# A wait of TensorE for its own transposes, and other places for three steps of VectorE and GpSimd in block 1

## The reference

```python
x = _layernorm(x + attention(x))          # first half, not touched
n = SU_ug.shape[0]
y = fwht(x * SU_ug) / SCALE               # 512-wide Hadamard transform of the tokens
up   = y @ W_up.T   * (Wscale_ug[:INTER] * SCALE)
gate = y @ W_gate.T * (Wscale_ug[INTER:] * SCALE)
y = fwht(silu(gate) * up * SU_dp) / SCALE # 2048-wide Hadamard transform
y = y @ W_down.T * (Wscale_dp * SCALE)
x = _layernorm(x + y)
```

## Time and profile before

| | |
|---|---|
| median of 3 runs | 1532.14 us |
| lowest, highest | 1530.12, 1534.98 us |
| the profiled execution, whole | 1534.02 us |
| its span, first to last instruction | 1532.2 us |
| mean granted TensorE clock | 0.997 |
| TensorE busy with matmuls | 1488.6 us, 97% |
| VectorE, ScalarE, GpSimd busy | 75%, 47%, 47% |

### The profile page before, as it was taken

How to read it: one execution, slowest core, us unless ns; L and a number is a source line. 1 busy time by engine, 2 the same in 40 slices (tenths; PEclk the granted TensorE clock), 3 DMA queues, 4 the chain that set the end, 5 groups by cost and what they waited for, 6 DMA issues and landing times.

```text
span 1532.2 us, 30672 instructions
## 1 busy us (share of the span) xinstructions
PE 1488.6 (97%) x11420; PEld 1394.1 (91%) x11420; DVE 1148.4 (75%) x1948; ACT 725.3 (47%) x1485; POOL 727.6 (47%) x861
## 2 busy tenths in 40 slices
PE   6999999999999999999999999999999999999998
PEld 4977988887887889899989999999999999999998
DVE  6776787677687886887886787688678677677665
ACT  4254245236227755444444455455455445545543
POOL 5465457438347553556663273264263254245122
PEclk9999999999999999999999999999999999999999
DMA  7022022122113797589779899899989988988981
GB/s 287 1 99 88 35 83 104 36 83 104 65 56 111 267 354 265 213 322 342 291 255 348 311 319 331 315 311 343 337 296 319 368 277 299 379 303 288 338 319 66
DMA packets 119298, 357.26 MB, mean 233 GB/s; under 512 B 12912, under 2 KB 13296, under 8 KB 117360
## 3 DMA queue, kind: packets, MB, share of 16 engines
q1 hardware_dynamic: 118144, 351.09, 63.5%
q10 hardware_dynamic: 1008, 4.20, 0.7%
HBM read 297.58 MB, written 57.67 MB: 232 GB/s over the span
## 4 chain that ended last, share of the span: by engine, by line
PE 58%; DVE 6%; issue 2%; ACT 2%; DMA 1%; POOL 1%; DVEq 0%; POOLq 0%; ACTq 0%
PE ff_acc L2517 16%; PE ff_bank_b L2486 16%; PE ff_bank_a L2486 10%; PE ff_bank_c L2486 10%; PE ff_acc L2551 1%; DVE ff_hs_a L2123 1%; PE ff_acc L2554 1%; DMA ff_pair_l<-low_scratch 1%; PE ff_x_ps L2445 1%; PE ff_x_ps L2434 1%; PE ff_x_ps L2457 1%; DVE ff_pair_l L2099 1%; PE ff_acc L2542 1%; DVE fb_h_lo L2118 1%; ACT at_union L601 1%
## 5 line engine op out<-in xcount | busy, mean ns | idle before, releaser
L2486 PE MATMUL ff_bank_b<-ff_x_hi,ff_ring 128*128 128x256 f32 x1536 | 299.1, 279 | 1.3 <-issue 0.6
L2486 PEld LDWEIGHTS ff_bank_b<-ff_x_hi,ff_ring 128*128 128x128 f32 x1536 | 247.8, 189 | 2.2 <-issue 1.8
L2486 PE MATMUL ff_bank_b<-ff_x_lo,ff_ring 128*128 128x256 f32 x768 | 214.2, 279 | 0.0
L1718 POOL TENSOR_TENSOR ff_h_sum<-ff_hf 128x256 f32<-128x256 f32 x54 | 40.6, 752 | 353.4 <-DVE ff_hf L2111 353.4
L2517 PE MATMUL ff_acc<-ff_pair_h,ff_hs_a 128*128 128x256 f32 x1080 | 201.4, 282 | 7.1 <-DVE ff_hs_a L2123 4.8
L2486 PE MATMUL ff_bank_a<-ff_x_hi,ff_ring 128*128 128x256 f32 x1024 | 201.5, 281 | 1.1 <-DVE ff_hf L2111 1.1
L2486 PE MATMUL ff_bank_c<-ff_x_hi,ff_ring 128*128 128x256 f32 x1024 | 202.0, 282 | 0.0
L2517 PEld LDWEIGHTS ff_acc<-ff_pair_h,ff_hs_a 128*128 128x128 f32 x1080 | 170.4, 190 | 9.2 <-DVE ff_hs_a L2123 5.8
L2486 PEld LDWEIGHTS ff_bank_c<-ff_x_hi,ff_ring 128*128 128x128 f32 x1024 | 165.3, 189 | 2.1 <-issue 2.1
L2486 PEld LDWEIGHTS ff_bank_a<-ff_x_hi,ff_ring 128*128 128x128 f32 x1024 | 165.3, 189 | 1.7 <-issue 1.6
L1883 ACT ACTIVATE ff_sg<-ff_c,h_ug_scale 128x512 f32<-128x512 f32 (+1 forms) x128 | 76.7, 614 | 158.7 <-DVE ff_c L2221 144.0
(11 more groups left out here) (369 smaller groups left out, 4243.2 us busy)
## 6 DMA issues: line engine op xcount, KB each, us to landing
ff_ring<-gu_scratch SPq DMA_DIRECT2D x392, 512.0 KB, 5.4
gu_scratch<-ff_ring SPq DMA_DIRECT2D x56, 512.0 KB, 4.3
ff_pair_l<-low_scratch SPq DMA_DIRECT2D x96, 256.0 KB, 3.7
ff_pair_more<-low_scratch SPq DMA_DIRECT2D x65, 256.0 KB, 3.6
at_xt<-in_xt SPq DMA_DIRECT2D x4, 2048.0 KB, 8.3
at_xn<-in_x SPq DMA_DIRECT2D x32, 256.0 KB, 2.9
x_scratch<-at_x SPq DMA_DIRECT2D x32, 256.0 KB, 2.0
fb_raw<-in_wgu SPq DMA_DIRECT2D x8, 1024.0 KB, 6.9
```

Of the source, the lines that this page charges most:

```text
L1718: pool.tensor_tensor(s1, a21, a22, ALU.add).then_inc(sum_s, 1)
L2486: i = pe.matmul(bank[:, m, :], r[:, a, m, c, :], b[:, k, c, :], start=(k < 3 and m == 0 and c == 0 and b is x_hi and a == 0), stop=(m == 1 ...
```

## The change

Three things are done. First, behind each turn of x in blocks 1 to 6 TensorE waits for the semaphore that the last of its own four transposes raises (24 places: six blocks, four turns). Second, GpSimd does `combine_down(2)` behind the sums of step 2 instead of ahead of the lo part for group 0, and `combine_down(3)` behind the three lo parts for group 2 instead of ahead of the one for group 1; the counts in `wd_summed` and `h_summed` follow. Third, VectorE makes the last lo part of the right operand of groups 0 to 3 (`lower_pair(q, 6)`) ahead of the first lo part of the left operand of the next group, instead of behind it.

```diff
         def wd_summed(n):
-            return sum_s, 4 * PAIRS + n + (0, 0, 8, 16)[(n - 1) // 4]
+            return sum_s, 4 * PAIRS + n + (0, 0, 12, 20)[(n - 1) // 4]
 
         def h_summed(n):
-            return sum_s, 4 * PAIRS + n + (8, 12, 16)[min((n - 1) // 8, 2)]
+            return sum_s, 4 * PAIRS + n + (8 if n <= 12 else 12 if n <= 20 else 16)
...
                 sum_h(blk, 1)
+                down_group(group_at(blk, 2))
+                sum_h(blk, 2)
                 if blk == 1:
                     combine_down(2)
-                down_group(group_at(blk, 2))
-                sum_h(blk, 2)
                 lower_three(group_at(blk, 4))
                 sum_h(blk, 3)
-                if blk == 1:
-                    combine_down(3)
                 down_group(group_at(blk, 4))
                 sum_h(blk, 4)
                 if blk < FBLK - 1:
                     pair_sums(blk + 1)
                 lower_three(group_at(blk, 6))
+                if blk == 1:
+                    combine_down(3)
                 sum_h(blk, 5)
...
                 at(blk, p, 12, last)
+                if q < 4:
+                    lower_pair(q, 6)
                 if not whole(blk, p):
                     lower_part(blk, p, 0)
-                if q < 4:
-                    lower_pair(q, 6)
                 add_down(q, 3)
...
                 for t in range(FT):
                     i = pe.transpose(x_ps[:, P * t:P * t + P], y[parity][:, t, P * c:P * c + P], ident[:, :])
                 i.then_inc(xt_ps.sem, 1)
+                if not folded:
+                    pe.wait_ge(*xt_ps.now(blk, c + 1))
```

## The result

| | before | changed |
|---|---|---|
| median of 8 runs | 1531.96 us | 1536.49 us |
| lowest, highest | 1528.30, 1534.98 | 1534.32, 1541.30 |
| ratio, 95% interval | | 1.0035 [1.0019, 1.0052] |
| profiled execution, span | 1534.02, 1532.2 | 1534.79, 1533.0 |

The change costs 5.4 us (2.9 to 8.0) where the forecast had +4.0. Its time of 1536.1 us is met within half a microsecond. The rest of this document shows that its terms were not met: by a fit to the times of the single edits three of them were off by 2 to 3 us each, in both directions, so that the total owes something to luck.

The account below looks back on a forecast made before the run. TensorE, with matmuls in flight for 97% of the span, was taken as the bound. Terms +7.4 - 1.5 - 0.8 + 0.3 - 0.5 - 0.9 = +4.0 us on 1532.1 gave 1536.1 us, own range 1532 to 1540, with rivals 1528.5 to 1542.

Parts of the forecast that it names:

- The wait behind the turns, 24 x 0.33 us: At 24 turns, TensorE's second matmul of the next product comes 0.33 us later each, 7.9 us in all.
- Net 7.4 us of it: Cost of the turn waits after taking off 0.5 us for turns where TensorE stops within two products anyway.
- Group 0, -1.5 us: Block 1, group 0: without GpSimd's combine_down(2) beside it, VectorE's lo pair ends earlier and TensorE's stop goes, -1.5 us.
- Group 1, -0.8 us: Block 1, group 1: without combine_down(3) beside it, the lo pair ends before TensorE is ready, -0.8 us.
- Other pairs, +0.3 us: Steps 3 and 5: moved sums lengthen other lo pairs by up to 1.6 us each; cost 0 to 3.2, booked 0.3 us.
- the -2.0 of the sums alone: The forecast's total for the two moved GpSimd sums in groups 0, 1 and the other pairs: -2.0 us, ratio 0.9987.
- The swap, -0.5 us: Group 3: TensorE's 1.34 us stop goes, but VectorE's equally long queue delays the next step's fourth product; 0.5 us stays.
- Half clock behind the 2.4 us stop "stays": Group 3's first product, early block 2: TensorE's 3.3 us at granted clock 0.52 behind the longest stop remain unchanged.
- Pace, -0.9 us: Matmul pace behind the turns, 240 us in six blocks: six in ten stretches fast, booked -0.9 us.
- no lock: Behind the turns the waits fix neither matmul pace; rivals gave always fast 0.17, and always slow (or doubled pairs holding TensorE) 0.18.
- The side, slower by a third of a per cent: Whole kernel: slower by over 0.3%, above 1536.7 us, given a chance of 0.39 in all.

Follow-up runs that it names:

- the twenty waits: Kernel before with only the 20 waits behind the turns of blocks 2 to 6, none in block 1: ratio 1.0027, +4.1 us.
- the passed waits: Kernel before with 24 waits at the changed kernel's places, but for a semaphore count reached long ago: ratio 1.0003.
- 48 waits: Kernel before with the 24 waits plus the same wait behind each multiplication of x by the Hadamard matrix, blocks 1 to 6: ratio 1.0109, +16.7 us.

## Why the prediction was right, and where it was not

If each edit counts for itself, the seven timed kernels made of them (the changed one, the waits, sums, swap, their two combinations, and the twenty waits as 20/24) give by least squares (95% bounds): waits +5.1 +- 1.4 us, sums +1.0 +- 1.7, swap -2.7 +- 1.5. They scatter more about this than their intervals allow (chi square 9.3 for 4), so these bounds are somewhat narrow. Farthest off are the sums alone (+1.0 by the fit, -1.4 measured) and the changed kernel (+3.4 and +5.4).

- *The wait behind the turns, 24 x 0.33 us*: the number of places and the price are right to 0.01 us, and the passed waits show that it is the end of the own transposes that is waited for. The forecast had it from the earlier trace rows. The 166 ns that the Trainium skill gives on the page "TensorE: Matmul & The Clock Gate" (they stand in its section "Single matmul latency") made an estimate of 4 us. The distances, 0.32 us each, go against that estimate.
- *Net 7.4 us of it*: over-sized for the median, 5.1. Absorbed in block 1 is 0.7 us (0.5 forecast). The remaining 2 us are open. The granted clock is not the reason: its mean over the runs is 0.9971 with the 24 waits and 0.9972 before, with the 20 waits 0.9976 and 0.9976. The pace is a candidate: its excess over 113.3 ns is 16.8 to 22.6 us in the six profiles with late waits, mean 19.5, and 19.9 to 26.3 us in the other eight, mean 22.6. But the stretch ahead of block 0, where all kernels are alike, also differs between those two groups, 519.5 against 517.7 us, in the other direction. One profile each can't settle this, and 48 waits came at full price.
- *Group 0, -1.5 us*: this step failed. The collision was rightly named and went, but the forecast did not ask what is late next within the group. That is the lo part for product 5, behind a store of the same buffers that takes longer than before, 0.78 us in the changed kernel, 1.02 in the sums alone and 1.30 in the sums with the swap.
- *Group 1, -0.8 us*: right at its place.
- *Other pairs, +0.3 us*: in the changed kernel 2.60 and 2.45 us stand against an expected 2.87 at most, and the first product of step 4 loses nothing beyond its own wait, as foreseen; some 0.6 us go at the next two places of step 4 (721.50 and 723.73), by the starts of matmuls. Without the waits the pair in step 3 takes 3.46 and 3.56 us, and TensorE stops 0.70 and 0.80 us. So the moved sums by themselves cost more than the term had. It was mis-sized further, since it ended there. Through the longer pair in step 5 GpSimd's later work comes later against VectorE's, and the two collide at group 2's end (0.97 us in the sums alone) or in step 0 of block 2 (1.0 us more in the changed kernel, whose pair there takes 3.40 us). By the stops this and group 0 turn the -2.0 of the sums alone into +0.3, by the starts of matmuls into +0.7, by the times into -1.4 to +1.0 with some 2 us to either side.
- *The swap, -0.5 us*: under-sized. The forecast took the queue of VectorE as equally long. By its stops the swap is worth 1.2 us and by the fit 2.7; the other 1.5 us are not accounted for. Some of it may be the clock. The runs of the swap alone had a mean granted clock of 0.9978, the kernel before beside them 0.9972. Within one kernel, over the 234 runs of the experiments, a run is some 1.15 us longer for each 0.001 less, which makes an estimate of 0.7 us.
- *Half clock behind the 2.4 us stop "stays"*: wrong in the changed kernel's profile. Behind a stop of 2.41 us the clock stays at its upper level, 2.4 GHz:

```profile
796.60:799.90 3.30, 3.30 (x30) 1.00 0.79 320
```

Ten of the fourteen profiles have a half-clock stretch behind that stop; the changed kernel, the waits alone, the sums with the swap and the waits with the swap have none. Whether it goes with the kernel or with the execution, one profile each does not tell. It is worth 1.6 us, half of the 3.3 us of the earlier trace rows.

- *Pace, -0.9 us*: no lock, as forecast. Over all profiles, the fast pace follows 114 of 196 turns without the wait and 73 of 140 with it.

So, by the fit, 7.4 was some 2 us too much, the sums cost 3 us more than forecast and the swap gave 2 us more. These errors nearly cancel, which was luck. (The fit's own sum is 3.4 us, 2 us below the 5.4 measured.) The side, slower by a third of a per cent, rests on the waits, and that part is shown.

## What to carry to other kernels

In this kernel a wait of TensorE for its own last result cost 0.33 us in a full stream, behind transposes as behind matmuls of 128x256; a wait for a count long reached cost nothing that could be seen. Work moved on a helper engine took its collision along even where it fitted into a gap: the operation beside it got longer, what waits for that came later, and one has to follow this until a slack has swallowed it. And of a stop that goes, ask what is late next in the same group, a store included. Where waits are summed over a stretch, see that its edge cuts the same stops in both kernels.

## What was not expected of the hardware

Back-to-back fp32r matmuls of 128x256 run at 113.3 or at 117.8 ns apart at the same granted clock, and the share of slow ones differs from 3754 of 8062 to 5851 of 8061 between profiles. Over the faster pace that is an excess of 16.8 to 26.3 us; the 9.5 us between these two is about the spread between runs of one kernel. What chooses the pace at a break is open. Two stops of equal length (2.43 and 2.41 us) were followed by a granted clock of 0.52 in one profile and 1.00 in another.
